# Two attention layers on one core: the statistics between the layers, the first high parts, and the first maxima of layer 1

## The reference, cut to what matters

```python
# x: (8, 512, 32, 32) float32: B = 8 images, C = 512 channels, N = 1024 places
# layer 0: linear attention, heads of 64 channels, 1x1 convolutions
K, Q, V = conv1x1(X, Wq, bq), conv1x1(X, Wk, bk), conv1x1(X, Wv, bv)   # then split into heads
M = einsum('bhmn,bhen->bhme', K, V)
Out = conv1x1(einsum('bhme,bhmn->bhen', M, Q), Wo, bo) + X
mean, var = Out.mean((0, 2, 3)), Out.var((0, 2, 3))                    # over the whole batch
x1 = (Out - mean) * rsqrt(var + EPS) * gamma + beta
# layer 1: softmax attention behind a group norm over 32 groups of 16 channels, per image
xn = (x1 - mean_g) * rsqrt(var_g + EPS) * gamma + beta
q, k, v = split(w_qkv @ xn + b_qkv)
a = softmax(q.T @ k / 8) @ v.T                                         # per head of 64
out = x1 + w_proj @ a + b_proj
```

## Time and profile before

| | |
|---|---|
| median of 3 runs | 2491.03 us (2490.61 to 2492.5) |
| profiled execution: time | 2492.64 us |
| profiled execution: span | 2491.1 us |
| busy share PE, DVE, ACT, POOL | 98%, 65%, 46%, 47% |
| mean granted TensorE clock | 0.99 of full speed |
| last product of layer 0 ends, first of layer 1 starts | 651.7 us, 666.5 us |

### The profile page before, as it was taken

How to read it: one execution, slowest core, us unless ns; L and a number is a source line. 1 busy time by engine, 2 the same in 40 slices (tenths; PEclk the granted TensorE clock), 3 DMA queues, 4 the chain that set the end, 5 groups by cost and what they waited for, 6 DMA issues and landing times. The chain is left out here.

```text
span 2491.1 us, 37555 instructions
## 1 busy us (share of the span) xinstructions
PE 2438.5 (98%) x12980; PEld 1615.9 (65%) x12980; DVE 1615.9 (65%) x2161; ACT 1150.5 (46%) x1499; POOL 1182.5 (47%) x590
## 2 busy tenths in 40 slices
PE   8999999999799999999999999999999999999988
PEld 7888888788655566557556655755665575557544
DVE  6455555455667766775777577567857756775776
ACT  3332233223355645654555456355555645553553
POOL 3330000000047665773766667377656755771762
PEclk8999999999899999999999999999999999999999
DMA  6431111013221242215122321512231241213002
GB/s 199 139 111 45 56 67 66 27 42 128 83 95 35 111 144 88 109 32 211 34 97 104 130 101 53 194 43 102 93 144 34 110 175 63 97 31 119 26 26 76
DMA packets 73401, 226.75 MB, mean 91 GB/s; under 512 B 12224, under 2 KB 12224, under 8 KB 72384
## 3 DMA queue, kind: packets, MB, share of 16 engines
q1 hardware_dynamic: 58720, 172.01, 19.6%
q0 software_dynamic: 14560, 52.96, 5.8%
HBM read 141.05 MB, written 71.30 MB: 85 GB/s over the span
## 5 line engine op out<-in xcount | busy, mean ns | idle before, releaser
L591 POOL TENSOR_TENSOR a_all<-a_all 128x1024 f32<-128x1024 f32 x410 | 1010.1, 2464 | 508.2 <-ACT a_all L816 473.3
L816 ACT ACTIVATE a_all<-psum 128x1024 f32<-128x1024 f32 x512 | 496.5, 1022 | 80.3 <-PE psum L1539 67.7
L1104 DVE TENSOR_REDUCE small<-psum 128x2 f32<-128x1024 f32 x326 | 399.6, 1226 | 172.3 <-PE psum L1509 172.1
L1558 PE MATMUL psum<-a_all 128*64 128x512 f32 x2048 | 495.7, 605 | 0.0
L1311 PE MATMUL psum<-r_all 128*128 128x512 f32 x1920 | 454.5, 395 | 6.9 <-DVE r_all L1198 5.8
L1311 PEld LDWEIGHTS psum<-r_all 128*128 128x128 f32 x1920 | 359.4, 189 | 101.6 <-DVE r_all L957 10.2
L1539 PE MATMUL psum<-r_all 64*128 64x512 f32 x3200 | 417.8, 393 | 2.0 <-ACT a_all L816 2.0
L1498 PE MATMUL psum<-r_all 128*128 128x512 f32 x1536 | 364.4, 396 | 5.6 <-DVE r_all L1217 5.6
L1539 PEld LDWEIGHTS psum<-r_all 64*128 64x128 f32 x3200 | 301.7, 186 | 73.2 <-ACT a_all L816 14.0
L1498 PEld LDWEIGHTS psum<-r_all 128*128 128x128 f32 x1536 | 286.0, 189 | 85.9 <-issue 24.4
L1558 PEld LDWEIGHTS psum<-a_all 128*64 128x64 f32 x2048 | 124.0, 136 | 232.5 <-issue 173.4
(11 more groups left out here) (147 smaller groups left out, 2450.9 us busy)
## 6 DMA issues: line engine op xcount, KB each, us to landing
r_all<-w_dram SPq DMA_DIRECT2D x48, 1024.0 KB, 4.9
xn_dram<-a_all POOLq DMA_DIRECT2D x56, 512.0 KB, 7.0
r_all<-xn_dram SPq DMA_DIRECT2D x7, 4096.0 KB, 15.3
a_all<-y_dram SPq DMA_DIRECT2D x9, 2048.0 KB, 10.8
a_all<-x SPq DMA_DIRECT2D x16, 1024.0 KB, 6.5
y_dram<-a_all SPq DMA_DIRECT2D x16, 1024.0 KB, 4.2
out<-a_all SPq DMA_DIRECT2D x32, 512.0 KB, 4.0
a_all<-sums SPq DMA_DIRECT2D x192, 64.0 KB, 2.0
```

What stands on the lines that cost most here:

```text
L591: pool.tensor_tensor(p_sum[:, :, cols], probs[:, 0, :, cols] if i == 1 else p_sum[:, :, cols], probs[:, i % SLOTS, :, cols], ALU.add).then ...
L816: act.activation(probs[:, i % SLOTS, :, cols], psum[half][:, :, :], ACT.Exp, scale=SCALE).then_inc(probs_ready, 1)
L1104: dve.reduce_max(max2[:, :, tile, half], psum[3][:, :, :], AX_X).then_inc(work_free, 2)
L1558: last = pe.matmul(psum[2][h * D:(h + 1) * D, half], v_t[:, i, head], probs[:, i % SLOTS, h, half * HALF:(half + 1) * HALF], start=(i == 0 ...
```

## The change

Four edits, all between the last image of layer 0 and the loop over layer 1.

- Statistics: the aggregates of a channel tile are made behind the count of the next tile in the last image's second half (`channel_stats`), with two fills and `nbk_c` behind the first count. The last image's means about the channel mean (`centred`) are made there too, so that `x1_mean` follows straight from the scale. Epsilon is given to ACT's root as its bias (`eps_c`), and to the Newton step by one operation of two (`inverse_root`). The roots' inputs are read where they stand, the second one in PSUM. `bn_bias`, the variances scaled, the bias less the group mean, `g1_scale` and `res_bias` stand after what TensorE or ACT waits for, beside their work.
- First high parts: ACT makes them from `y_first` with scale and bias itself, without DVE. DVE writes the normed values to `x_first`, in slots 0 and 1 of `probs`, and waits for the last stores of `y32` first.
- Unread products: `keep_pace` makes 8 products of 128 x 512 into bank 5 ahead of the first average's wait, and 10 behind the second average. Nothing reads them.
- First maxima: two score tiles stand behind one another, one in `psum[3]` and one in `psum[2]`, once in each v tile (after the third channel tile's products in the first, after the first's in the last, after the second's in the others). A tile waits for the maximum of the one two before (n - 4). Ahead of the first, TensorE waits for both halves of the queries and the second of the keys.

```diff
@@ -128,12 +128,13 @@
...
         y_first = v_t.rearrange("p (j h) n -> p j (h n)", j=CT)
+        x_first = probs[:, 0:2].rearrange("p a h n -> p (a h) n")
         p_sum = a1.take(2, N)
...
-        SMALL = 676
+        SMALL = 680
...
@@ -143,9 +144,9 @@
...
         bn_mv = s.take(CT, 2)
-        bn_var = s.take(CT)
+        g1_scale = s.take(CT)
         gn_in = s.take(CT, B)
-        gn_mean = s.take(CT, B)
+        centred = s.take(CT, B)
         gn_tmp = s.take(CT, B)
...
@@ -154,6 +155,7 @@
...
         unused = s.take(CT)
+        eps_c = s.take(1)
         nbk_c = s.take(CT)
...
@@ -208,7 +210,6 @@
...
         norm_ready = sem("norm_ready")
-        var_ready = sem("var_ready")
         root_ready = sem("root_ready")
...
@@ -255,6 +256,13 @@
...
+        def wide(v):
+            return v.unsqueeze(2).to_broadcast([P, CT, B])
+
+        def group(i):
+            return bank(6 + i)[:, 0:CT * B].rearrange("p (j b) -> p j b", b=B)
+
+        gn_root = root_tmp.rearrange("p (j b) -> p j b", b=B)
         T0, U0, A0, RING0 = NT, NT + CT, NT + 2 * CT, NT + 3 * CT
...
@@ -673,8 +681,8 @@
...
                 cols = slice(half * HALF, (half + 1) * HALF)
-                act.wait_ge(xn_made, u + 1)
-                act.activation(xn[:, HI, j, cols], y_first[:, j, cols], ACT.Copy).then_inc(xn_hi_done, 1)
+                act.activation(xn[:, HI, j, cols], y_first[:, j, cols], ACT.Identity, scale=xn_scale[:, j, 0:1],
+                               bias=xn_bias[:, j, 0:1]).then_inc(xn_hi_done, 1)
...
@@ -745,15 +753,17 @@
...
-            for i, (v, root) in enumerate(((bn_var, bn_scale), (gn_in, gn_tmp))):
-                act.wait_ge(var_ready, i + 1)
-                act.activation(root, v, ACT.Sqrt).then_inc(root_ready, 1)
+            act.wait_ge(stats_ready, CT * (B + 1))
+            act.activation(bn_scale, bn_mv[:, :, 1], ACT.Sqrt, bias=eps_c).then_inc(root_ready, 1)
+            act.wait_ge(gn_averaged, 2)
+            act.activation(gn_root, group(1), ACT.Sqrt, bias=eps_c).then_inc(root_ready, 1)
...
             act.wait_ge(norm_ready, 1)
+            act.wait_ge(y_first_loaded, 16)
             for u in range(FIRST_MADE):
...
@@ -874,6 +884,23 @@
...
+            steps = FIRST + B * STEPS
+
+            def then(ins):
+
+                nonlocal steps
+                steps += 1
+                ins.then_inc(dve_step, 1)
+                dve.wait_ge(dve_step, steps)
+
+            def channel_stats(j):
+
+                dve.wait_ge(y_counted, B * NH * CT - CT + j + 1)
+                dve.bn_aggr(bn_mv[:, j], stats[:, j].rearrange("p a k -> p (a k)")).then_inc(stats_ready, 1)
+                dve.bn_aggr(mean_var[:, j, B - 1], stats[:, j, (B - 1) * NH:B * NH].rearrange("p a k -> p (a k)")).then_inc(stats_ready, 1)
+                dve.wait_ge(stats_ready, CT * (B - 1) + 2 * (j + 1))
+                then(dve.tensor_scalar(centred[:, j], mean_var[:, j, :, 0], bn_mv[:, j, 0:1], None, ALU.subtract))
+
...
@@ -999,6 +1026,13 @@
...
                         dve.bn_stats(to, y32[:, h, o]).then_inc(y_counted, 1)
+                        if last and h == 1:
+                            if o == 0:
+                                then(dve.memset(max_cols, 0.0))
+                                then(dve.memset(eps_c, EPS))
+                                then(dve.tensor_scalar(nbk_c, bqkv_c[:, CT:2 * CT], -1.0, None, ALU.mult))
+                            else:
+                                channel_stats(o - 1)
                     if h == 0 and not last:
...
@@ -1008,61 +1042,40 @@
...
-
-            steps = FIRST + B * STEPS
-
-            def then(ins):
-
-                nonlocal steps
-                steps += 1
-                ins.then_inc(dve_step, 1)
-                dve.wait_ge(dve_step, steps)
-
-            def invert(root, v, tmp):
+            def inverse_root(root, v, tmp):
...
                 then(dve.tensor_tensor(tmp, root, root, ALU.mult))
-                then(dve.tensor_tensor(tmp, tmp, v, ALU.mult))
+                then(dve.scalar_tensor_tensor(out=tmp, in0=v, scalar=EPS, in1=tmp, op0=ALU.add, op1=ALU.mult))
                 then(dve.tensor_scalar(tmp, tmp, -0.5, 1.5, ALU.mult, ALU.add))
...
-            def wide(v):
-                return v.unsqueeze(2).to_broadcast([P, CT, B])
-
-            dve.wait_ge(y_counted, B * NH * CT)
-            for j in range(CT):
-                dve.bn_aggr(bn_mv[:, j], stats[:, j].rearrange("p a k -> p (a k)")).then_inc(stats_ready, 1)
-            batch_stats(B - 1)
-            dve.wait_ge(stats_ready, CT * (B + 1))
-            dve.tensor_scalar(bn_var, bn_mv[:, :, 1], EPS, None, ALU.add).then_inc(var_ready, 1)
+            channel_stats(CT - 1)
             dve.wait_ge(root_ready, 1)
-            invert(bn_scale, bn_var, root_tmp[:, 0:CT])
+            inverse_root(bn_scale, bn_mv[:, :, 1], root_tmp[:, 0:CT])
             then(dve.tensor_tensor(bn_scale, bn_scale, g0_c, ALU.mult))
+            then(dve.tensor_tensor(x1_mean, centred, wide(bn_scale), ALU.mult))
+            dve.tensor_tensor(x1_mean, x1_mean, wide(b0_c), ALU.add).then_inc(gn_moved, 1)
+
+            x1_var = xn_scale
             then(dve.tensor_tensor(bn_bias, bn_mv[:, :, 0], bn_scale, ALU.mult))
             then(dve.tensor_tensor(bn_bias, b0_c, bn_bias, ALU.subtract))
+            then(dve.tensor_tensor(x1_var, mean_var[:, :, :, 1], wide(bn_scale), ALU.mult))
+            then(dve.tensor_tensor(x1_var, x1_var, wide(bn_scale), ALU.mult))
+            dve.wait_ge(gn_moved, 1)
+            dve.wait_ge(gn_averaged, 1)
+            then(dve.tensor_tensor(gn_tmp, x1_mean, group(0), ALU.subtract))
+            then(dve.tensor_tensor(gn_tmp, gn_tmp, gn_tmp, ALU.mult))
+            dve.tensor_tensor(gn_in, x1_var, gn_tmp, ALU.add).then_inc(gn_moved, 1)
+            then(dve.tensor_tensor(xn_bias, wide(bn_bias), group(0), ALU.subtract))
+            then(dve.tensor_tensor(xn_bias, xn_bias, wide(g1_c), ALU.mult))
+            then(dve.tensor_tensor(g1_scale, bn_scale, g1_c, ALU.mult))
             then(dve.tensor_tensor(res_bias, bn_bias, bp_c, ALU.add))
-            then(dve.tensor_tensor(x1_mean, mean_var[:, :, :, 0], wide(bn_scale), ALU.mult))
-            dve.tensor_tensor(x1_mean, x1_mean, wide(bn_bias), ALU.add).then_inc(gn_moved, 1)
-            dve.wait_ge(gn_moved, 1)
-
-            dve.wait_ge(gn_averaged, 1)
-            then(dve.tensor_copy(gn_mean, bank(6)[:, 0:CT * B].rearrange("p (j b) -> p j b", b=B)))
-
-            then(dve.tensor_tensor(gn_tmp, x1_mean, gn_mean, ALU.subtract))
-            then(dve.tensor_tensor(gn_tmp, gn_tmp, gn_tmp, ALU.mult))
-            then(dve.tensor_tensor(gn_in, mean_var[:, :, :, 1], wide(bn_scale), ALU.mult))
-            then(dve.tensor_tensor(gn_in, gn_in, wide(bn_scale), ALU.mult))
-            dve.tensor_tensor(gn_in, gn_in, gn_tmp, ALU.add).then_inc(gn_moved, 1)
-            dve.wait_ge(gn_averaged, 2)
-            dve.tensor_scalar(gn_in, bank(7)[:, 0:CT * B].rearrange("p (j b) -> p j b", b=B), EPS, None, ALU.add).then_inc(var_ready, 1)
+            dve.wait_ge(gn_moved, 2)
             dve.wait_ge(root_ready, 2)
-            invert(gn_tmp, gn_in, root_tmp.rearrange("p (j b) -> p j b", b=B))
-            then(dve.tensor_tensor(gn_tmp, gn_tmp, wide(g1_c), ALU.mult))
-            then(dve.tensor_tensor(xn_scale, gn_tmp, wide(bn_scale), ALU.mult))
-            then(dve.tensor_tensor(xn_bias, wide(bn_bias), gn_mean, ALU.subtract))
-            then(dve.tensor_tensor(xn_bias, xn_bias, gn_tmp, ALU.mult))
-            then(dve.memset(max_cols, 0.0))
-            dve.tensor_scalar(nbk_c, bqkv_c[:, CT:2 * CT], -1.0, None, ALU.mult)
+            inverse_root(gn_root, group(1), gn_tmp)
+            then(dve.tensor_tensor(xn_scale, gn_root, wide(g1_scale), ALU.mult))
+            then(dve.tensor_tensor(xn_bias, xn_bias, gn_root, ALU.mult))
             dve.tensor_tensor(xn_bias, xn_bias, wide(b1_c), ALU.add).then_inc(norm_ready, 1)
...
@@ -1097,11 +1110,11 @@
...
-            def max_tile(m):
+            def max_tile(m, of=psum[3]):
...
                 dve.wait_ge(work_full, work.pair(m))
-                dve.reduce_max(max2[:, :, tile, half], psum[3][:, :, :], AX_X).then_inc(work_free, 2)
+                dve.reduce_max(max2[:, :, tile, half], of[:, :, :], AX_X).then_inc(work_free, 2)
...
@@ -1206,19 +1219,24 @@
...
             dve.wait_ge(y_first_loaded, 16)
+            for h in range(NH):
+                dve.wait_ge(y_stored[h], B * 16)
             for u in range(NH * CT + 1):
...
                     j, cols = u % CT, slice(u // CT * HALF, (u // CT + 1) * HALF)
-                    dve.tensor_scalar(y_first[:, j, cols], y_first[:, j, cols], xn_scale[:, j, 0:1], xn_bias[:, j, 0:1],
-                                      ALU.mult, ALU.add).then_inc(xn_made, 1)
+                    dve.tensor_scalar(x_first[:, u // 2, u % 2 * HALF:(u % 2 + 1) * HALF], y_first[:, j, cols], xn_scale[:, j, 0:1],
```

(53 more changed lines are left out.)

## The result

The changed kernel takes 2502.4 us (median of 6 runs, 2500.4 to 2514.4) against 2492.0 (6 runs, 2490.6 to 2492.8): 1.0056 of the time, 95% interval 1.0037 to 1.0075. It is slower by 10 us where I had forecast 8 us less.

What follows compares the result with a forecast made beforehand. TensorE, busy in 98% of the span, bounds the kernel, so only its waits and slowed products count. Terms of 4.2 + 3.4 + 0.8 = 8.4 us, taken as 8.2, from the median 2491.0 gave 2482.8; range 2480.8 to 2487.0.

Steps and rivals of the forecast that it cites:

- 1729 of 1746 us, and nothing there is edited: Layer 1, from 713.8 to 2460 us: TensorE is busy for nearly all of it, so earlier edits only move that stage.
- Rival (d): Clock falls in layer 1's first products and stays down through the v tiles: slower by 5 us, 2508 at most; chance 0.04.
- Eighteen products fill 651.7 to 653.6: Between the layers: the unread products fill that pause and the time behind the second average, to hold the clock; worth 0.2 us.
- So they delay nothing: Ten unread products from 657.7 end at 662.1, before the first low part at 662.2, so cost nothing, by a thin margin.
- last count to first reciprocal: Statistics after layer 0's last output tile: three of each aggregate lie in DVE's pauses, reciprocal at 654.1 instead of 655.85, 1.75 us.
- to second reciprocal: Statistics, second average to reciprocal: ACT reading the average itself takes out DVE's epsilon step, 0.2 us of 1.15.
- first low part to v tiles: Layer 1's first products: first low part 4.15 us earlier, query tiles 4.2 us earlier, the middle of 4.35 and 4.0.
- v tiles and turn: V products with maxima in twos gain 3.4 us; TensorE's wait before the maxima are joined falls from 1.7 to 0.9, 0.8 us.
- Rival (b): First root kept back behind its table load by another 1.28 us: statistics give 1.15 us less, 2483.9; chance 0.07.
- A round of v and maxima: V tiles: two score pairs behind one another, then twelve products, take 3.53 us instead of 4.03; eight rounds gain 3.4 us.
- the better case: Clock full for layer 1's first products: query tiles end 4.35 us earlier, against 4.0 with the first 5.3 us at half pace.
- rival (c): Gain given back later, as stretches of half clock like the last batch's fall otherwise: 2487, no change; chance 0.13.

## Why the prediction was wrong

**The step that failed** is the one that I had not written down as a sum: "1729 of 1746 us, and nothing there is edited; what comes before 713.8 only moves that stage." It moves the stage in time, and I took that for all. It also moves TensorE's loop in its code, by 37 instructions, from place 188 to 225 of a block, and this costs 20 us (2502.4 against 2482.2 at place 190). My rivals held no such case. Rival (d), slower, was built on the clock; the clock did fall in layer 1, but not in the v tiles: it fell behind the waits for code, and added to their price. The terms that I counted as free, "Eighteen products fill 651.7 to 653.6" and "So they delay nothing", were right about their time and left out that each is two instructions of code ahead of a loop. That a code fetch can hold TensorE up was to be read in none of the earlier trace rows; the queue of instruction packets in the profile (97 of them, 16 KB each) did say that code streams in during the whole kernel.

**The edited part**, step by step, from the changed kernel's trace:

| step | forecast gain, us | measured | how |
|---|---|---|---|
| last count to first reciprocal | 1.75 | 0.8 | 653.13 to 655.85 before, 653.57 to 655.51 after |
| to first average | 0.6 | 0.6 | 2.26 to 1.68 |
| first to second average | 0.55 | 0.65 | 2.12 to 1.46 |
| to second reciprocal | 0.2 | 0.05 | 1.15 to 1.10 |
| tail to the norms | 0.75 | 0.8 | 1.42 to 0.64 |
| norms to first low part | 0.3 | 0.2 | 1.54 to 1.32 |
| first low part to v tiles | 0.05 | 0.35 | 14.38 to 14.02 |
| v tiles and turn | 4.2 | 3.8 | 33.83 to 30.00 |
| sum | 8.4 | 7.25 | |

The first term was mis-read, not mis-measured. The aggregates of channel tile o - 1 stand *behind* the count of tile o, so that behind the last count come two channels' worth, at 653.49 and 654.43, not one: two of each lie in DVE's pauses, where I had three. The table load had 1 us to spare (it ends at 654.07, the root's inputs at 655.08). Rival (b) falls all the same: held back by another 1.28 us behind the load, the root could have started at 655.35 at the earliest, and it started at 655.12. A round of v and maxima takes 3.60 us (685.68 to 689.28), 3.53 forecast; the four products of half the rows take the 0.66 of the forecast, the twelve full ones 2.94 and not 2.87. From the second average to the second reciprocal only 0.05 of 0.2 us came: the root, which now reads PSUM, takes 0.29 us (0.23 before), and the reciprocal starts 0.42 behind the root's start (0.26 before). TensorE's idle time ahead of the turn is 0.99 us instead of 1.61. With the unread products the clock was full in the stretch from 664 to 668 already, as I took for the better case.

With its loop at 190 the changed kernel takes 2482.2 us, 9.4 less than its runs of before (interval 5.5 to 11.7); the trace explains 7 of them. That this is so near the 8.2 of the forecast is in part luck, since the edited part gained 1.15 less than its sum. The rest lies behind the turn: 1774.4 us from turn to end at 190, 1777.3 in the profiled execution of before, 1774.8 in that of the kernel before at 190, with passes of 223.3 us in all three. What differs are the spells of half clock in the last pass and the last image, as rival (c) had it, in both directions. The profiled executions can't say whether the other 2 us belong to the change: the medians of before and after with the loop at 190 lie 9.3 apart, their profiled executions 6.9.

**The better version** is the changed kernel with its loop at place 190: 0.9966 of before, and 20 us under the changed kernel as it stands.

## What to carry to other kernels

Code ahead of a long loop is not free when its work is hidden: it moves the loop in its blocks of code, and a loop whose code is fetched anew in each pass can lose microseconds at every edge when it comes to lie over one block more. So compare the time from pass to pass of the loops that a change doesn't touch, look for waits on "issue" at their first products, and count code packets per pass; and fix the head's place where the language can, before parts are measured one by one. Filler work is to be counted in instructions as well as in microseconds. And the loop's length is to be counted in the trace: here the code's count missed 288 of 2600.

## What was not expected of the hardware

- TensorE's loop of ten blocks and 40 instructions touches eleven or twelve blocks. A head at place 227 or 235 of a block costs a twelfth fetch of 16 KB per pass and 10 or 17 us over six edges, its own place (225 by the second wait) 20; at 0, 100, 190 and 210 there is none.
- The transfer engines are busy throughout ahead of the edge in both kernels: DMA share 1.03 at 412 GB/s in the 4 us ahead of it before, 1.02 at 413 after. A code fetch there stands beside data. Whether it would take less time with idle ones was not tried.
- In the profiled execution of the changed kernel four of the six edges, with waits of about 2 us ahead of the turn, were followed by spells of half clock, five in all; two edges with the same wait were not. Waits of about 1 us, as at place 227 of the changed kernel, were followed by none in its own.
